# Two causal attentions: 64-row half tiles, maxima at row 63, and a new order of a group's matmuls

## The reference, cut to what matters

```python
# layer 0
scores = einsum('bhid,bhjd->bhij', q, k) / sqrt(hd)
std_out = out_proj(softmax(where(mask, scores, neg)))
gsa_scores = scores + position_sensitivity * splat_attn     # rank 16 more: 8 splats, two features each
gsa_out = out_proj(softmax(where(mask, gsa_scores, neg)))
out = (1 - blend) * std_out + blend * gsa_out
# layer 1
scores = einsum('bqhd,bkhd->bhqk', q, k) * scale
out = einsum('bhqk,bkhd->bqhd', softmax(where(causal, scores, min)), v)
```

## Time and profile before

| | us |
|---|---|
| median of 3 runs | 2149.99 |
| lowest, highest of the 3 | 2125.07, 2183.54 |
| the profiled execution | 2145.68 |
| its span, first to last instruction | 2143.8 |
| mean granted TensorE clock of the span | 0.857 |

### The profile page before, as it was taken

One profiled execution on the slowest core, in us unless ns is written; L12 is line 12 of the kernel. 1 busy time (PEld: TensorE's weight loads), 2 busy tenths in 40 slices (PEclk: granted clock), 3 DMA queues, 4 the chain that ended last, 5 costly groups with the idle time before them and its releaser, 6 DMA issues. The chain is left out here.

```text
span 2143.8 us, 32204 instructions
## 1 busy us (share of the span) xinstructions
PE 1855.6 (87%) x10498; PEld 1261.3 (59%) x10498; DVE 1549.8 (72%) x3465; ACT 1289.5 (60%) x2904; POOL 587.3 (27%) x1144
## 2 busy tenths in 40 slices
PE   4988899999999888788888988887778699997998
PEld 3557444545445377666667776666656344436787
DVE  7655766878777266999997789999446678835554
ACT  2533456767667633799986679998523277775111
POOL 2002011122112203545553445455123011113400
PEclk9999566989878899888879998888979599988999
DMA  2453131332231010000000000000015423101000
GB/s 109 158 157 60 30 60 31 61 61 53 38 61 31 2 66 1 1 1 1 1 1 1 1 1 1 1 1 1 0 44 143 102 55 61 37 2 66 1 1 40
DMA packets 36133, 82.53 MB, mean 38 GB/s; under 512 B 9600, under 2 KB 11776, under 8 KB 34944
## 3 DMA queue, kind: packets, MB, share of 16 engines
q1 hardware_dynamic: 35968, 80.48, 15.4%
HBM read 52.79 MB, written 27.26 MB: 37 GB/s over the span
## 5 line engine op out<-in xcount | busy, mean ns | idle before, releaser
L1030 ACT ACTIVATE probs<-pss 128x512 f32<-128x512 f32 (+3 forms) x1152 | 489.2, 493 | 233.7 <-PE pss L993 228.3
L1058 DVE TENSOR_REDUCE negmax<-px 128x2 f32<-128x1024 f32 (+2 forms) x480 | 515.3, 1114 | 148.2 <-PE px L974 145.6
L993 PE MATMUL pss<-queries,keys 49*128 49x512 f32 (+3 forms) x1152 | 335.8, 437 | 19.0 <-ACT probs L1030 12.1
L974 PE MATMUL px<-keys,queries 48*128 48x512 f32 (+3 forms) x1152 | 298.5, 470 | 11.5 <-DVE negmax L1058 7.5
L1563 POOL TENSOR_SCALAR rp<-sw,tau 128x256 f32<-128x256 f32 x576 | 275.5, 507 | 63.7 <-DVE st L1709 56.6
L993 PEld LDWEIGHTS pss<-queries,keys 49*128 49x128 f32 x1152 | 191.8, 216 | 166.4 <-ACT probs L1030 114.0
L1007 PE MATMUL po<-probs,vals 128*32 128x512 f32 (+3 forms) x2304 | 278.8, 580 | 2.2 <-POOL probs L1106 1.2
L1391 PE MATMUL pt<-ident,sw 128*128 128x128 f32 x768 | 160.5, 350 | 114.0 <-ACT sw L1474 70.1
L1462 ACT ACTIVATE ra<-sw,neg 128x256 f32<-128x256 f32 x576 | 243.6, 519 | 1.6 <-DVE neg L1685 1.6
L1106 POOL TENSOR_SCALAR_AFFINE_SELECT probs<-probs 128x512 f32<-128x512 f32 x192 | 120.8, 637 | 429.4 <-ACT probs L1030 429.4
L1406 PE MATMUL pss<-again,sw 128*128 128x256 f32 x1024 | 236.5, 394 | 0.0
(11 more groups left out here) (352 smaller groups left out, 2610.7 us busy)
## 6 DMA issues: line engine op xcount, KB each, us to landing
queries<-rec_q SPq DMA_DIRECT2D x96, 128.0 KB, 3.5
keys<-rec_k SPq DMA_DIRECT2D x96, 128.0 KB, 3.7
queries<-rec_q SPq DMA_DIRECT2D x96, 64.0 KB, 3.5
keys<-rec_k SPq DMA_DIRECT2D x96, 64.0 KB, 3.5
rec_q<-fs SPq DMA_DIRECT2D x16, 256.0 KB, 4.5
rec_k<-fs SPq DMA_DIRECT2D x16, 256.0 KB, 4.8
rec_q<-vals SPq DMA_DIRECT2D x16, 256.0 KB
rec_k<-vals SPq DMA_DIRECT2D x16, 256.0 KB
```

The lines of the kernel that those rows point to most:

```text
L974: x = e.matmul(px[:, n, s * width:(s + 1) * width], ops.qs[p][at:at + STACK, tile, t * P:(t + 1) * P], ops.ks[p][at:at + STACK, tile, c:c ...
L993: e.matmul(tl.pss[scores % 3][:, 512 - width:512], ops.ks[p][at:at + STACK + 1, tile, j * P:(j + 1) * P], ops.qs[p][at:at + STACK + 1, til ...
L1030: e.activation(tl.probs[arg][:, w, :], tl.pss[scores % 3][:, 512 - width:512], ACT.Exp).then_inc(self.exp_made, 1)
L1058: e.tensor_reduce(out, from_px, X_AXIS, ALU.max, negate=True).then_inc(self.x_read, 1)
```

## The change

- `STACK` becomes `HALF - 1`, 63. So `m` runs over 63 rows in place of 48, `s` over 64 in place of 49, and the row of maxima moves from row 48 to row 63 of each half tile (the same DMA, another partition). DMAs of the records stay at their 48 rows.
- Rows 48 to 62 of the queries have now to be zero: each tile of queries is filled with 0.0 by one more memset ahead of that of its keys, at all four places. In these rows the keys hold 1.0. SP's waits count two memsets for each tile.
- `ORDERS`: both strings are new, with the same letters (20 m, 48 s, 12 v, and r, two d, two t).
- An assertion at build time that a gsa maximum falls on the `px` tile of its std maximum; it adds no instruction.

```diff
-STACK = 48
+STACK = HALF - 1
...
         for p in range(t.early):
+            e.memset(f32(t.qs[p][:]), 0.0).then_inc(self.made, 1)
             e.memset(f32(t.ks[p][:]), 1.0).then_inc(self.made, 1)
...
         for p in range(t.early):
-            e.wait_ge(self.made, p + 1)
+            e.wait_ge(self.made, 2 * (p + 1))
             t.load(self.k, e, p)
...
-    ORDERS = {1: "msmssmsvsmsmssvvdsmsmssssmsssmsmssvsmmssvsmssvmssdvsmsmvsssmvssmsmvsmssvsssvrtssstsss", 2: "mmsssmsmmsssvvmssmsssmsssmsdsmssvmsssmvmssvvdmssmsvsmssvssmstsstsmssmssvmsssvvrssvsss"}
+    ORDERS = {1: "mmsssvmssmsvmsssmvsmsssmsssdmssstsmssmvmsssmvsmsvvdssmsmvsssmvmsssmvssmsvsssrtsssvsss", 2: "mmssvmsmssvmssmsvsmsssmsmsssvsmdsssmvsmssmvsmssvsmsvsmssdmsmssvmsssmvsssvrsssttsssvss"}
...
                 if g < 3:
-                    e.wait_ge(self.place_made, g + 1 - tl.early)
+                    e.wait_ge(self.place_made, 2 * (g + 1 - tl.early))
...
         for p in range(self.ops.early, 3):
+            e.memset(f32(self.ops.qs[p][:]), 0.0).then_inc(self.place_made, 1)
             e.memset(f32(self.ops.ks[p][:]), 1.0).then_inc(self.place_made, 1)
...
-                e.wait_ge(self.cleared, 1)
+                e.wait_ge(self.cleared, 2)
                 ops.load(k, e, 0)
...
+        e.memset(f32(ops.qs[0][:]), 0.0).then_inc(self.cleared, 1)
         e.memset(f32(ops.ks[0][:]), 1.0).then_inc(self.cleared, 1)
```

More of the change, by code:

```diff
@@ L947, in pe @@
         k, tl, ops = self.k, self.t, self.ops
-        places, scores, maxed = 0, 0, -1
+        places, scores, maxed, std_place = 0, 0, -1, {}
         for what, g, w, arg in self.units:
@@ L962, in pe @@
                 fresh = not ops.adds(w)
+                if fresh:
+                    std_place[arg] = places
+                else:
+                    assert places == std_place[arg] + 2
                 if diag and fresh:
```

## The result

| | before | after |
|---|---|---|
| median of 4 runs, us | 2140.17 | 2031.82 |
| lowest, highest | 2125.07, 2183.54 | 2029.85, 2033.48 |
| span of the profiled execution | 2143.8 | 2028.1 |

The ratio is 0.9525, its 95% interval 0.9462 to 0.9589. The forecast was 2075 with a range down to 2042: the direction and the place were right, and the gain was half as large again (108 us between the medians where 71 were forecast, 115.7 between the spans). Not only the median moved: the runs of before lie 58 us apart, those of after 3.6.

A forecast was written before the change was run, and what follows sets the result against it. TensorE and its clock were taken to bound the attention groups. 64 (first attention's clock) + 3 (second's) + 4 (order) = 71 us less than the profiled 2145.7 gave 2075 us, range 2042 to 2128.

The forecast's parts named there:

- Place and bound: Both attentions: only they can move; TensorE and its clock set a group's length, no engine full alone at 1.00.
- Rows cost nothing: `m` and `s` matmuls in both attentions: more rows do not lengthen them, costed at 0.
- The clock: First attention: rows and strings together keep the clock up within groups, 64 us less; second attention 3 us less.
- neither edit reaches the clock: Rival: low clock stays at 40% of the first attention, only the order's 4 us gained, 2142 us; chance 0.14.
- The prediction's account of the strings: Both attentions: new strings shorten most stretches without sums; the first's longest run goes from 18 units to 11.
- The first group: First attention: its first group starts at the low clock, 10.3 us too long; 8 us of this ramp stay.
- The string at the full clock: First attention: 1.3 us a group off for VectorE's gap behind `r` against 1.1 of splits; 4 us less.
- the splits: First attention: three double sums a group become single, 0.26 to 0.36 us each, 12 to 17 us in all.
- The second attention: 3 us less by the clock (1.5 from its one slow group), and 0 within 4 for its string.
- The last groups: Second attention's last group, 35.4 us at 0.76: a fifth of 7 us may go; nothing put on the first's.
- Memsets: Six more on GpSimd, 1.8 us each, hidden behind other work; at most 1 us on the next addition to x.
- the order term: First attention's new string at the full clock: 4 us less, between 17 more and 24 less.

The follow-up runs named there:

- e7: The changed kernel with VectorE's maxima of single-tile chunks taken over half of the columns only; 2013.76 us.
- e8: The changed kernel with the two old order strings and maxima of single-tile chunks over half of the columns; 2055.63 us.
- e14: The changed kernel with each exponential over half of its columns, maxima whole; 2020.35 us.
- e15: The changed kernel with the two old order strings and each exponential over half of its columns; 2052.81 us.
- e12: The changed kernel with both maxima and exponentials over half of their columns; 1984.55 us.
- e13: The changed kernel with the two old order strings and both maxima and exponentials over half of their columns; 2018.43 us.
- e1: The changed kernel (63 and 64 rows) with the two old order strings; 2069.64 us, ratio 0.9723 to the kernel before.
- e2: The kernel before (48 and 49 rows) with the two new order strings; 2037.80 us, ratio 0.9569.
- e9: The changed kernel with the old order strings and 55 and 56 rows in place of 63 and 64; 2093.64 us.
- e6: The changed kernel, first string with maxima at the old string's places and all other letters in the new order; 2118.50 us.
- e3: As e1, but in the first string the two turns stand together behind the rows of maxima; 2086.60 us, ratio 0.9803.
- e4: As e1, but each of the first string's three double sums is split by a score; 2090.37 us, ratio 0.9817.
- e11: The changed kernel with the two new order strings exchanged between the attentions; 2062.80 us.
- e5: The changed kernel, first string with maxima at the new string's places and all other letters in the old order; 2143.09 us.

## Why the prediction was right or wrong

- **Place and bound: right, with a limit.** A group's length was set by TensorE and its clock, and at the full clock no engine was full alone. Halving one engine's work gives at most 0.3 us in the first attention (e7, e8, e14, e15), halving both gives 1.3 to 1.4 (e12, e13).
- **Rows cost nothing: right.** TensorE's busy time in a full-clock group is 26.39 us in the earlier trace rows and in e1, with 15 rows more in 96 matmuls.
- **The clock: right in size, with the cause shared otherwise than thought.** Forecast 64 us in the first attention; the rows alone gave 67.7. "Together they keep the clock up" was not quite how it is: either does nearly all of it alone, e1 and e2. The case that neither edit reaches the clock is out, and with it the reading that only idling matters: TensorE was no busier in e1 than before. The Trainium skill (TensorE: Matmul & The Clock Gate, What's actually happening) has idling bring the throttle and activity release it; the rows of e1, e9 and the earlier trace rows show more than that, since 48, 55 and 63 rows gave three clocks at the same sequence of matmuls. The prediction's account of the strings, that they work by shortening the stretches without sums, is not borne out as it stands: e6 has nearly the same stretches and filled rows, and 0.92.
- **The first group.** I left 8 us of its excess. With the old strings (e1) it took 31.9 us, 4.6 over the others, and that explains 3.4 of the 3.7 us by which the rows' 67.7 exceeds my 64. With the new ones it took 27.9, 2.0 over, though its clock was 0.71 as against 0.74.
- **The string at the full clock: the step that failed.** "I take 1.3 us a group off (the gap behind `r`, less its latency) against the 1.1 us of the splits: about 0.25 a group, **4 us less**". The difference is 0.2, and 1.1 is the upper end of my own 0.26 to 0.36 a split. The term of the splits was measured at 0.9 in the old string and stands. The other, taken from VectorE's gap behind the rows of maxima, has no base: e3 filled that gap and lost 0.7 us. At the full clock the string gives 1.4 us a group, 19.3 us in 14 groups, where I had 0.25. Where it saves them I had not costed at all, neither in TensorE's sequence nor in how the turn-round of PSUM tiles is hidden; e12 and e13 do not part these two, so the cause stays open.
- **The second attention: mis-sized.** I put 0 within 4 for its string, as it has as many runs of sums. It gives 1.1 us in each of the 6 full groups between e1 and after (6.8 us), 10.4 us in all from the first to the last cast (203.2 to 192.8), and 4.2 more in the last group (32.8 to 28.6). Counting runs of sums was the wrong measure in both strings. Of what I gave the clock there, 3 us, the slow group's 1.5 came as forecast.
- **The last groups.** I had put nothing on the first attention's and 1.4 us on the second's. They gave 3.0 and 5.7 us.
- **The sum, part by part.** The clock, as the rows alone hold it, was forecast at 67 us and gave 75.4 (67.7 and 3.7 between casts, 2.5 and 1.5 in the last groups). The strings on top of it were forecast at 4 us and gave 38.4: 26.1 in the 20 groups at the full clock, and 12.3 in the first and last group of each attention, where the clock is below 1.00. The first string's share, 23.8, just kept to the bound of 24; the second's, 14.6, was far beyond its 4.
- **Memsets: right.** Six more, 1.8 us each, and the first cast came at 229.0, before it was at 229.4. Ahead of the first attention the four memsets start at 163.91, 165.66, 167.41 and 169.17 us, 1.81 us each, and the addition to x follows at 170.94.
- **The median.** I set the new median equal to the sum, since groups would all be alike; the 3.6 us between runs bear that out. The old spread goes with the clock: of the runs of before beside e1 to e4, three took 2121.5 to 2124.7 us at a mean clock of the span of 0.868 to 0.870, and one 2145.0 at 0.858. By (1 - clock) / 0.5 that is 53 us more at the low level, or 21 us at 0.4 each (an estimate), of the 23.5 between the fastest and this one. Which groups fell in which execution is not shown, since one execution alone has a trace.
- **The range.** It ended at 2042 and the time was 2031.8. I had taken its low end from the order term's end and the ramp alone (20 and 10 us under 2075), and gave the second attention none of it.

## What to carry to other kernels

Where TensorE is busy throughout and its granted clock is still low, look at what runs there: matmuls that fill few rows of the array, with few full ones among them. Filling unused rows with zeros costs a memset if operands stay in place; another order costs no instruction, but it can lengthen a group. Try both, and expect that they don't add up, and that neither holds the clock in every order: e3 to e6, e8 and e11 had filled rows and falls.

A hand-written order of units is fitted as a whole. Features that the better order visibly has (single sums, late turns, even maxima) each made things worse by themselves, so cost an order by its full-clock group from a trace, not by its features, and give it a wide range of both signs: here 25.9 to 30.5 us for the same 85 units.

## What the runs showed of the hardware

- The granted clock rose with the number of rows that the stationary and moving operands span, though the added rows were zero on one side: 0.80, 0.93, 0.98 at 48, 55 and 63 rows with one and the same order of matmuls.
- With the rows filled, it still depended on the order: 0.98 after and in e1, 0.92 in e6, 0.89 in e5.
- Matmuls of 63 rows take what those of 48 take: in a full-clock group the 24 maxima of 512 columns took 467 ns each before and 466 in e1, the 24 scores 437 with 49 rows and 436 with 64.
- With the same matmuls, and VectorE and ScalarE relieved of a third of their work each, two orders still differ by 1.3 us in 25. The order of matmuls has a price beyond their columns; whether it is TensorE's own or that of the turn-round of PSUM tiles is not shown.
